# Both halves of the weighted values in one run of TensorE, output transfers on the scalar queue, pieces rearranged

## The reference: two layers of cross attention

```
q = x @ Wq + bq                      32 heads of 16
k = ctx @ Wk + bk; v = ctx @ Wv + bv  8 key/value heads of 16, each shared by 4 query heads
scores = q . k / 4 + mask
attn = softmax(scores)               over the 375 context rows
o = attn . v
x = layernorm(o @ Wo + bo + x) * gamma + beta
```

## Time and profile before

| | us |
|---|---|
| median of 3 runs | 1861.51 |
| lowest, highest | 1860.53, 1864.62 |
| the profiled execution's own time | 1861.11 |
| its span | 1859.3 |
| TensorE busy (of the span) | 1790.2 (96%) |
| VectorE busy | 1369.7 (74%) |
| ScalarE busy | 1034.4 (56%) |
| GpSimd busy | 573.1 (31%) |

### The profile page before, as it was taken

One profiled execution on the slowest core, in us unless ns is written; L12 is line 12 of the kernel. 1 busy time (PEld: TensorE's weight loads), 2 busy tenths in 40 slices (PEclk: granted clock), 3 DMA queues, 4 the chain that ended last, 5 costly groups with the idle time before them and its releaser, 6 DMA issues.

```text
span 1859.3 us, 36378 instructions
## 1 busy us (share of the span) xinstructions
PE 1790.2 (96%) x11521; PEld 1143.8 (62%) x11521; DVE 1369.7 (74%) x1808; ACT 1034.4 (56%) x1762; POOL 573.1 (31%) x1165
## 2 busy tenths in 40 slices
PE   2899899999999999999999999999999999999995
PEld 1666666666666666666666666666666666666651
DVE  4577677777777777777777777777777777777773
ACT  1355556556556556655655655655655565565552
POOL 1233233333323323323323323333332332333321
PEclk7899999999999999999999999999999999999997
DMA  6334544434434434434434434443443443443321
GB/s 254 104 121 162 151 122 136 131 121 138 131 118 139 130 118 140 132 115 141 132 117 141 132 109 132 127 123 118 129 127 109 132 129 109 132 128 122 119 69 36
DMA packets 200892, 235.91 MB, mean 127 GB/s; under 512 B 41706, under 2 KB 176100, under 8 KB 199812
## 3 DMA queue, kind: packets, MB, share of 16 engines
q1 hardware_dynamic: 200836, 235.19, 40.7%
HBM read 101.39 MB, written 22.02 MB: 66 GB/s over the span
## 4 chain that ended last, share of the span: by engine, by line
PE 90%; SPq 4%; DMA 2%; issue 2%; ACT 1%; POOL 1%; DVE 0%; ACTq 0%; POOLq 0%
PE ms L737 17%; PE pv L756 16%; PE sc L720 15%; PE job L798 12%; PE job L820 11%; PE job L774 9%; PE pv L786 8%; SPq L294 2%; DMA beta<-in_beta 1%; ACT probs L497 1%; PE pv L811 1%; DMA qs<-qp 0%; PE job L765 0%; ACT mT L511 0%; POOL kp L455 0%
## 5 line engine op out<-in xcount | busy, mean ns | idle before, releaser
L610 DVE TENSOR_REDUCE mx<-ms 112x2 f32<-112x750 f32 x1024 | 933.0, 932 | 432.3 <-PE ms L737 419.1
L497 ACT ACTIVATE probs<-sc 125x896 f32<-125x896 f32 x768 | 705.4, 919 | 423.2 <-PE sc L720 417.6
L737 PE MATMUL ms<-ks,qs 96*112 96x375 bf16 x2048 | 501.5, 326 | 20.7 <-DMA qs<-qp 18.3
L720 PE MATMUL sc<-qs,ks 99*125 99x448 bf16 x1536 | 428.5, 360 | 16.8 <-ACT probs L497 10.1
L737 PEld LDWEIGHTS ms<-ks,qs 96*112 96x112 bf16 x2048 | 254.9, 131 | 234.7 <-issue 108.9
L756 PE MATMUL pv<-probs,vs 125*32 125x448 f32 x3072 | 319.3, 549 | 0.0
L798 PE MATMUL job<-wo,on 128*112 128x512 f32 x512 | 269.8, 609 | 7.2 <-POOL on L439 5.7
L720 PEld LDWEIGHTS sc<-qs,ks 99*125 99x125 bf16 x1536 | 184.5, 137 | 148.4 <-ACT probs L497 89.0
L820 PE MATMUL job<-xT,wq 128*128 128x112 f32 x2048 | 250.1, 276 | 0.0
L820 PEld LDWEIGHTS job<-xT,wq 128*128 128x128 f32 x2048 | 245.5, 193 | 3.5 <-issue 0.6
L453 POOL TENSOR_TENSOR kr<-kf,kp 128x375 f32<-128x375 f32 x64 | 57.7, 901 | 546.8 <-ACT kp L527 518.2
(11 more groups left out here) (54 smaller groups left out, 1000.4 us busy)
## 6 DMA issues: line engine op xcount, KB each, us to landing
ctxT<-in_ctxT SPq DMA_DIRECT2D x64, 750.0 KB, 5.8
qs<-qp SPq DMA_DIRECT2D x768, 56.0 KB, 2.4
ks<-kp SPq DMA_DIRECT2D x768, 46.9 KB, 2.5
osum<-oraw SPq DMA_DIRECT2D x128, 112.0 KB, 2.6
oc<-oraw SPq DMA_DIRECT2D x128, 112.0 KB, 2.6
mask<-in_mask SPq DMA_DIRECT2D x64, 164.1 KB, 2.3
xT<-in_xT SPq DMA_DIRECT2D x32, 224.0 KB, 6.3
xin<-in_x SPq DMA_DIRECT2D x32, 224.0 KB, 6.6
```

The lines of the kernel that those rows point to most:

```text
L497: nc.scalar.activation(probs[0:KCS, k, :, :], sc[0:KCS, :, 0:GL], ACT.Exp)\
L610: nc.vector.tensor_reduce(mx[o][:, 2 * j:2 * j + 2], ms[j % 2][0:S, :, 0:S2], AX_X, ALU.max)\
L720: last = nc.tensor.matmul(sc[0:KCS, j, 0:GL], ks[p][0:KM, g, rows], qs[p][0:KM, g, :], start=True, stop=not masked)
L737: last = nc.tensor.matmul(ms[j % 2][0:S, n, 0:S2], qs[o][0:KT, g, S * c:S * c + S], ks[o][0:KT, g, :], start=True, stop=True)
```

## The change

- PAIRS_AT: piece 1 has one pair of maxima instead of two, piece 2 has two instead of one.
- TensorE computes both halves of the weighted values of post in piece 0, one behind the other, half 0 into pv and half 1 into job. Piece 7 no longer has a half of main.
- ScalarE copies half 0 before exp 0 and half 1 after it. Exp 0 and exp 1 wait for half 0 and half 1; exp 6 no longer does.
- The four transfers from oraw are issued by ScalarE: two behind the copy of half 1, two behind exp 1. They are gone from SyncE's list, in both places.
- The third and fourth group of the queries are projected in pieces 6 and 7 (before: both in 6). ScalarE evacuates the queries behind exp 7 (before: exp 6), and casts their second part behind exp 9 (before: 8).
- max_columns for the unit ahead moves from piece 7 to piece 8 and from job to pv, with its copy. The first head group of the output stays in piece 8, but behind both pairs of maxima.
- VectorE does centred and result_rows directly behind the statistics in piece 0 (before: in piece 4).

The waits for the banks follow. The diff, cut:

```diff
-PAIRS_AT = [2, 2, 1, 2, 0, 1, 1, 1, 2, 2, 1, 1]
+PAIRS_AT = [2, 1, 2, 2, 0, 1, 1, 1, 2, 2, 1, 1]
...
-            def outputs(p, h, value):
-                sp.wait_ge(pv_evac[p][h], value)
-                sp.dma_start(osum[64 * h:64 * h + 64, :], oraw[h][1::2, :]).then_inc(sum_in[p], 16)
-                sp.dma_start(oc[64 * h:64 * h + 64, :], oraw[h][0::2, :]).then_inc(o_in[p], 16)
...
-                if m_ok:
-                    outs = count(main + 1)
-                    if p_ok:
-                        weighted = count(2 * post + 2)
                 if a_ok:
                     load_mask(o, ahead, lay[1])
                     stack_terms(o, 1, ks[o], kp[o], 1)
-                if p_ok:
-                    outputs(o, 1, count(post + 1))
                 if a_ok:
                     stack_terms(o, 1, qs[o], qp, 0)
...
                     stack_terms(p, 0, qs[p], qp, 0, of=(0,))
-                if m_ok:
-                    if p_ok:
-                        sp.wait_ge(on_ready[o], weighted)
-                    outputs(p, 0, outs)
                 if a_ok:
                     max_rows(o, 0, count(2 * ahead + 1))
...
-                    if k == 0 and p_ok:
-                        act.wait_ge(pv_ps[o], 2 * post + 1)
-                    if k == HALF and p_ok:
-                        act.wait_ge(pv_ps[o], 2 * post + 2)
+                    if k < 2 and p_ok:
+                        act.wait_ge(pv_ps[o], 2 * post + 1 + k)
                     nc.scalar.activation(probs[0:KCS, k, :, :], sc[0:KCS, :, 0:GL], ACT.Exp)\
                       .then_inc(exp_done[p], 1)
-                def pv_out(u, h, n, before):
-                    act.wait_ge(pv_ps[u], 2 * n + h + 1)
-                    if before is not None:
-                        need(act, sum_in[1 - u], 32 * before)
-                        need(act, o_in[1 - u], 32 * before)
-                    nc.scalar.copy(oraw[h][:, :], pv[:, 0:GL]).then_inc(pv_evac[u][h], 1)
+                def pv_out(h):
+                    act.wait_ge(pv_ps[o], 2 * post + h + 1)
+                    if s_ok:
+                        act.wait_ge(sum_in[p], 32 * (stored + 1))
+                        act.wait_ge(o_in[p], 32 * (stored + 1))
+                    nc.scalar.copy(oraw[h][:, :], (pv, job)[h][:, 0:GL]).then_inc(pv_evac[o][h], 1)
+
+                def outputs(h):
+                    if s_ok:
+                        act.wait_ge(on_ready[p], 2 * stored + 2)
+                    act.wait_ge(pv_evac[o][h], post + 1)
+                    act.dma_start(osum[64 * h:64 * h + 64, :], oraw[h][1::2, :]).then_inc(sum_in[o], 16)
+                    act.dma_start(oc[64 * h:64 * h + 64, :], oraw[h][0::2, :]).then_inc(o_in[o], 16)
 
                 def m_out(u, h, n, before):
                     act.wait_ge(mt_ps[u], 2 * n + h + 1)
                     if before is not None:
                         need(act, m_rows[before[0]][1 - h], 16 * before[1])
-                    nc.scalar.copy(mT[:, :], job[0:PARTS * HH, 0:S]).then_inc(mt_evac[u], 1)
+                    nc.scalar.copy(mT[:, :], (pv, job)[h][0:PARTS * HH, 0:S]).then_inc(mt_evac[u], 1)
 
                 for k in range(PIECES):
+                    if k == 0 and p_ok:
+                        pv_out(0)
                     exp(k)
                     if k == 0 and p_ok:
-                        pv_out(o, 1, post, post + o)
+                        pv_out(1)
+                        outputs(0)
+                    if k == 1 and p_ok:
+                        outputs(1)
...
-                    if k == 6 and j_ok:
+                    if k == 7 and j_ok:
                         act.wait_ge(q_ps[p], proj + 1)
...
-                    if k == 7 and m_ok:
-                        pv_out(p, 0, main, main + p if p_ok else None)
-                    if k == 7 and a_ok:
+                    if k == 8 and a_ok:
                         m_out(o, 0, ahead, (p, main + 1) if m_ok else None)
-                    if k == 8 and j_ok:
+                    if k == 9 and j_ok:
                         for h in range(2):
                             cols = slice(GL // 2 * h, GL // 2 * (h + 1))
                             act.wait_ge(q_r[p], 2 * proj + h + 1)
...
                                 deviation()
+                                centred()
+                                result_rows()
                             if k == 2 and step == 0 and a_ok:
                                 values()
-                            if k == 4 and s_ok:
-                                centred()
-                                result_rows()
...
-                    job_free = [(o_evac[p], stored + 1) if s_ok else (mt_evac[p], 2 * main + 1) if m_ok else None]
+                    job_free = [(o_evac[p], stored + 1) if s_ok else (q_evac[o], NG * (ahead + 1)) if a_ok else None]
...
-                    def values(u, h, n):
-
-                        if h == 1:
-                            pe.wait_ge(pv_evac[u][0], n + 1)
+                    def values(h):
+
+                        if h == 0:
+                            pe.wait_ge(v_ready[o], post + 1)
+                            pe.wait_ge(mt_evac[p] if m_ok else mt_evac[o], 2 * main + 1 if m_ok else 2 * post + 1)
                         else:
-                            pe.wait_ge(v_ready[u], n + 1)
-                            if s_ok and lay[4] == 0:
-                                pe.wait_ge(yT_ready[p], stored + 1)
-                            elif j_ok:
-                                pe.wait_ge(k_evac[p], proj + 1)
-                            elif p_ok:
-                                pe.wait_ge(pv_evac[o][1], post + 1)
+                            take_job_bank()
                         for chunk in range(KC):
-                            pe.wait_ge(exp_done[u], PIECES * n + HALF * h + 2 * chunk + 2)
+                            pe.wait_ge(exp_done[o], PIECES * post + HALF * h + 2 * chunk + 2)
                             for j in range(4):
-                                last = nc.tensor.matmul(pv[32 * j:32 * j + 32, 0:GL],
-                                                        vs[u][:, chunk, 4 * h + j, :, :].rearrange("s d two -> s (d two)"),
+                                last = nc.tensor.matmul((pv, job)[h][32 * j:32 * j + 32, 0:GL],
+                                                        vs[o][:, chunk, 4 * h + j, :, :].rearrange("s d two -> s (d two)"),
                                                         probs[0:KCS, HALF * h + 2 * chunk + j // 2, j % 2, :],
                                                         start=(chunk == 0), stop=(chunk == KC - 1))
-                        last.then_inc(pv_ps[u], 1)
+                        last.then_inc(pv_ps[o], 1)
+                        if h == 1:
+                            job_free[0] = (pv_evac[o][1], post + 1)
 
                     def max_columns(u, h, n):
-                        take_job_bank()
+                        if h == 1:
+                            take_job_bank()
+                            job_free[0] = (mt_evac[u], 2 * n + 2)
+                        elif s_ok and lay[4] == 0:
+                            pe.wait_ge(yT_ready[p], stored + 1)
+                        elif j_ok:
+                            pe.wait_ge(k_evac[p], proj + 1)
+                        elif p_ok:
+                            pe.wait_ge(pv_evac[o][0], post + 1)
                         pe.wait_ge(m_part[u], 4 * (2 * n + h + 1))
-                        nc.tensor.matmul(job[:, 0:S], mwide[:, :], negident[:, :],
-                                         start=True, stop=True).then_inc(mt_ps[u], 1)
-                        job_free[0] = (mt_evac[u], 2 * n + h + 1)
+                        nc.tensor.matmul((pv, job)[h][:, 0:S], mwide[:, :], negident[:, :], start=True, stop=True)\
+                          .then_inc(mt_ps[u], 1)
...
-                                pe.wait_ge(pv_evac[o][1], post + 1)
+                                pe.wait_ge(pv_evac[o][0], post + 1)
+                            elif m_ok:
+                                pe.wait_ge(mt_evac[p], 2 * main + 1)
...
-                            pe.wait_ge(pv_evac[o][1], post + 1)
+                            pe.wait_ge(pv_evac[o][0], post + 1)
...
                         if k == 0 and p_ok:
-                            values(o, 1, post)
+                            values(0)
+                            values(1)
...
                         if k == 6 and s_ok and lay[4] == 0:
                             transpose_rows()
                         if k == 6 and j_ok:
-                            project_queries((2, 3))
-                        if k == 7 and m_ok:
-                            values(p, 0, main)
-                        if k == 7 and a_ok:
+                            project_queries((2,))
+                        if k == 7 and j_ok:
+                            project_queries((3,))
+                        if k == 8 and a_ok:
```

(4 more changed lines are left out.)

## The result

The changed kernel takes 1918.2 us (median of 4 runs, 1917.4 to 1919.3) against 1862.5 (median of 4): 1.030 times the time before, 95% interval 1.028 to 1.032, 55.7 us. 1915 was forecast.

The account below looks back on a forecast made before the run. TensorE's order of work and waits bound the kernel, with ScalarE the bound in some pieces. Savings of 0.25 and 0.25 against stalls of 0.98 and 0.36 gave +0.86 us a slot, 53 over 62 slots: 1915 us, range 1884 to 1966.

Parts of the forecast that it names:

- One run of values, -0.25: Piece 0, TensorE: entering and leaving the run of values once instead of twice saves 0.25 us a slot.
- Job bank, -0.25: First output product: no longer waits for mT to leave the job bank, saving 0.25 us a slot.
- Evacuation of the queries, +0.98: Piece 8: score product 9 waits for exp 8, 3.29 us against 2.31 of TensorE work, costing 0.98 a slot.
- The last query transfers, +0.36: Next slot's first maxima product: waits for the later-cast query transfers, 0.36 us a slot, bounds 0 to 1.0.
- the rule: Score product k+1 ends no sooner than exp k's end plus 0.65 us, because of the single sc buffer.
- Issues on ScalarE, 0: Output transfers issued by ScalarE run beside its compute instructions and cost 0, between 0 and +1.0 us a slot.
- The rival in which they stand in line: ScalarE's four issues hold up exp 1 and exp 2, +0.61 us a slot, 1952 us; chance 0.24.
- its strong form: Two queues take turns, so outputs(0) takes 2.45 instead of 1.2 and product 2 is delayed: +0.98 a slot, 1975 us.
- Layer norm rows on VectorE, 0: Piece 0: the moved rows' 1.49 us fit before the later second maxima product, costing nothing.
- The sum: All terms together: +0.5 and +0.36 give +0.86 us a slot, 53 us over 62 slots, 1915 us.
- faster: Queries' evacuation does not hold exp 8, so only the savings remain: -0.5 a slot, 1830 us; chance 0.11.
- No wait for the stack: Query transfers land in time since SyncE is emptier: +0.5 a slot, 1892 us; chance 0.16.

Follow-up runs that it names:

- The cut run: Changed kernel with the second maxima product of piece 0 placed between the two halves of the weighted values: 1940.0 us, ratio 1.0401.
- the exchange: Kernel before with two ScalarE copies of piece 7 exchanged, mT's ahead of that of half 0: 1848.6 us, ratio 0.9932.
- the early casts: Changed kernel with the casts of the queries' second part behind exp 8 instead of exp 9: 1910.1 us, ratio 1.0260.
- three repairs: Changed kernel with, separately, queries' evacuation and first casts on VectorE (1903.6 us), both piece 0 maxima pairs behind the values (1926.2), second casts one piece earlier (1910.1).

## Why the prediction was right

**One run of values, -0.25.** The first run enters with 2.39, the second follows with 2.25, one long row is gone: 0.14 + 0.10. The cut run confirms it with 0.28 by its rows (0.34 by the times, with another wait in it). Right.

**Job bank, -0.25.** 0.20 by the exchange in the kernel before. In the changed kernel nothing of it is to be seen, since the first output product waits for the evacuation of the queries there, inside the stall of piece 8, as the prediction had it. That wait is larger than its 0.25, though: on VectorE, where exp no longer waits, 0.6 of the stall stayed.

**Evacuation of the queries, +0.98.** 3.28 from the queries' end to the end of score product 9 in one slot and 3.35 in the next (1432.11 to 1435.46), against the 3.29 worked out from before, with 2.31 of work. This is the term that decides the sign. Three runs carry it: more ScalarE work there is paid nearly in full, none there takes TensorE's wait for exp away (though only 0.4 of the 0.98, since the bank holds the rest), and the same stall appears in the kernel before once its run is moved.

**The last query transfers, +0.36.** Last issue at 1437.59, landing 1440.53, product at 1440.65 to 1441.17. Score product 0 ended 0.65 after the end of exp 11 (1438.96 + 0.92, by the rule), at 1440.53, so the pair would have ended at 1440.85: 0.32. Right in place and nearly in size. What I had not seen is that SyncE's queue is at most 0.27 behind the cast: the prediction says under its rivals that the cast and not the queue sets the landing, and the early casts gained 8 us and not 18.

**Issues on ScalarE, 0.** They lie beside the copy and exp 1. The rival in which they stand in line (1952) is refuted by the rows, and so is its strong form: ScalarE's issues from 1417.69 to 1418.82 lie inside a row of six back-to-back issues of SyncE (1415.14, 3.96 long, where six took 3.78), and the medians of ScalarE's issues are 0.47 and 0.62, those of SyncE for the same two transfers before 0.52 and 0.60, so nothing doubled. The Trainium skill's page "Perfetto Trace Analysis" (DMA Instruction, HWDGE) has the descriptor generator locked for one issuer at a time. If so, the lock was held only rarely when ScalarE came: of 128 issues of oc the longest took 1.67. Going back to SyncE made this kernel 5 us faster all the same, but not in its slots (1653.10 against 1652.60 for 58 of them): in the slots 0 is right. 1.3 of the 5 us is seen at the program's end, and the rest stays open.

**Layer norm rows on VectorE, 0.** Right that no wait arises at the second maxima product, wrong in what they take: y took 1.68 on average instead of 0.78. VectorE is late into pieces 1 to 3, and the second maxima product of piece 3 takes 0.41 for 0.32 (in the chain above); TensorE's loads waited 28.3 us for reductions between 200 and 1750 us, 17.5 before:

```profile
PEld ms L728 <- DVE mx L602: 28.3, 77, 0.5
```

```profile
PEld ms L737 <- DVE mx L610: 17.5, 56, 0.3
```

The first of these lines is the changed kernel's. That is 0.09 a slot in the chain shown, which the prediction had put at nothing. Whether y or the pair moved from piece 1 to piece 2 makes it is not shown; no run has one without the other.

**The sum.** For the slot shown, with 3.35 - 2.31 = 1.04 in piece 8: -0.24 - 0.25 + 1.04 + 0.32 + 0.09 = +0.96, and it is 28.26 against 27.31, 0.95 longer. It is one of the longer ones; over the 58 slots the mean is +0.79, where the forecast had +0.86. The terms are right, then, each within a tenth. That 1915 came so near to 1918 owes something to luck: 62 slots of 0.79 are 49, and nearly 7 of the 55.7 us lie at the ends of the program, which the prediction had put at 0 to within 3. Part of them is in the chain at the end: the program ends on both runs of the last unit, 2.39 + 2.30, where it had one of 2.44 (its last slot gives back 1.5), and the sums land 4.42 behind the last run where they landed 3.11 behind it. Slots a little shorter than forecast and ends that are longer lie on opposite sides.

Of the rivals, "faster" asked that exp 8 start within 0.7 of the queries' end; it started 1.70 after (1405.69 against 1403.99). "No wait for the stack" is refuted by the chain.

## What to carry to other kernels

When work is moved between engines' fixed lists, ask what it was covering: TensorE's 2.4 us of values in piece 7, with 1.2 of its other work, hid 3.3 us of ScalarE between two score products, and 0.5 us of real savings elsewhere could not pay for the hole. Price a chain from the event that starts it to the next product that needs it, and set the bound engine's work between the same two events against it; the shares of busy time (54% and 94% here) say nothing of it. After one wait is removed look for the next in the same place before the gain is booked: here SyncE's queue came at most 0.3 us behind the cast, the job bank kept 0.6 of the stall when the exp was out of the way, and the four banks of ms took over from the transfers. Each of three repairs gave back half or more of what it removed.

## What the runs showed of the hardware

- Transfers issued by ScalarE run beside the activation ahead of them: the issue of 0.47 starts 0.06 after the start of a copy of 0.53, and the next activation, whose scores were ready 0.5 before, starts 0.1 after the issues' end.
- Element-wise work on VectorE and on GpSimd can draw each other out. Moved to piece 0, y on VectorE runs while GpSimd does res, and y is drawn out; the lines of y in the kernel before and then in the changed one (busy, mean ns) follow. GpSimd's rstd, now beside VectorE's zg and no longer beside a reduction, went from 571 to 989 ns.

```profile
L655 DVE SCALAR_TENSOR_TENSOR y<-zg,rstd,beta 112x512 f32<-112x512 f32 x64 | 50.1, 782 | 11.1 <-DVE zg L646 6.4 <-POOL rstd L445 1.3
```

```profile
L647 DVE SCALAR_TENSOR_TENSOR y<-zg,rstd,beta 112x512 f32<-112x512 f32 x64 | 107.6, 1681 | 32.2 <-POOL rstd L429 32.2
```

  Each kernel has slots that do it the other way round, and they part the instruction from its neighbour. First the kernel before, in which only the last two y have a res beside them (here at 1840.82, 1.26 long); then the changed kernel, in which only the last y has none:

```profile
1840.89 1.74 DVE L655 SCALAR_TENSOR_TENSOR y<-zg,rstd,beta 112x512 f32<-112x512 f32 x1 [0.44 <-POOL rstd L445]
```

```profile
1911.91 0.75 DVE L647 SCALAR_TENSOR_TENSOR y<-zg,rstd,beta 112x512 f32<-112x512 f32 x1 [0.44 <-POOL rstd L429]
```

  Only the one that starts later is drawn out: res (1416.67) keeps its 1.27 and y (1416.73) takes 1.76; zg (1415.55) keeps its 0.74 and rstd (1415.71) takes 0.99.
- A stall of TensorE can cost more than its length: after 3.5 us with 1.7 busy, the next 4 us were granted 0.57 of full speed, and 2.39 of work took 4.09. It need not: in another slot of the same run 3.5 us with 1.67 busy (from 1230.30) were followed by 4.4 us at 1.00. In the changed kernel, whose stalls are a microsecond, the clock stayed at 1.00.
